# A macaron block with routed experts: a first stage of four tiles from one quarter of the tokens, and the front in another order

## The reference

```python
x = x + 0.5 * ffn(layernorm(x), ...)
x = x + attn(layernorm(x), ...)          # element [1] of it: a linear recurrence, 3 layers
x = x + 0.5 * ffn(layernorm(x), ...)

def ffn(x, Wr, br, ln_g, ln_b, W1, b1, W2, b2):        # E = 8 experts, D = 256, F = 1024
    router_probs = softmax(xt @ Wr + br)
    gates, idx = max(router_probs), argmax(router_probs)
    xn = layernorm(xt) * ln_g + ln_b
    h = relu(xn @ W1[idx] + b1[idx])
    return (h @ W2[idx] + b2[idx]) * gates
```

## Time and profile before

| what | value |
|---|---|
| median of 3 runs (lowest, highest) | 724.63 us (719.66, 725.75) |
| the profiled execution, its own time | 724.52 us |
| its span | 722.7 us |
| mean granted TensorE clock | 0.95 of full |
| PE busy, PEld busy | 665.7 us (92%), 582.8 us (81%) |
| DVE, ACT, POOL busy | 407.8, 269.7, 171.8 us |
| moved by DMA | 126.51 MB, 175 GB/s over the span |

### The profile page before, as it was taken

One profiled execution on the slowest core, in us unless ns is written; L12 is line 12 of the kernel. 1 busy time (PEld: TensorE's weight loads), 2 busy tenths in 40 slices (PEclk: granted clock), 3 DMA queues, 4 the chain that ended last, 5 costly groups with the idle time before them and its releaser, 6 DMA issues.

```text
span 722.7 us, 15480 instructions
## 1 busy us (share of the span) xinstructions
PE 665.7 (92%) x4414; PEld 582.8 (81%) x4414; DVE 407.8 (56%) x1415; ACT 269.7 (37%) x640; POOL 171.8 (24%) x177
## 2 busy tenths in 40 slices
PE   5748999799999999999998989999899989999993
PEld 4437899699997887888777867889699979999992
DVE  7356684233355667687787667787567623333331
ACT  3214222223234568453662546644343213222220
POOL 4452334111111111123412240123212511111111
PEclk8557999999999999999999999999999999999997
DMA  8897573765464552434515437333464465453540
GB/s 285 252 377 270 175 236 132 255 223 210 159 207 153 186 189 97 150 133 152 193 54 194 147 115 264 124 105 111 148 236 143 143 225 182 165 166 133 158 140 14
DMA packets 59919, 126.51 MB, mean 175 GB/s; under 512 B 8105, under 2 KB 36660, under 8 KB 59700
## 3 DMA queue, kind: packets, MB, share of 16 engines
q1 hardware_dynamic: 53204, 108.50, 44.6%
q0 software_dynamic: 6624, 16.92, 6.5%
HBM read 106.36 MB, written 20.35 MB: 175 GB/s over the span
## 4 chain that ended last, share of the span: by engine, by line
PE 63%; DVE 10%; issue 8%; SPq 5%; DVEq 4%; DMA 4%; POOL 2%; another core or an unknown queue 1%; ACT 1%; POOLq 0%; ACTq 0%
PE bank L1629 28%; PE bank L1643 26%; PE bank L1616 2%; SPq L403 2%; DMA pay<-routed_rows 2%; POOL routed_rows L609 2%; SPq L440 1%; PE bank L1533 1%; DVEq L391 1%; DMA routed_rows<-rows,dest 1%; DVE rec L1023 1%; PE bank L1566 1%; PE bank L1471 1%; DVE act_t L1113 1%
## 5 line engine op out<-in xcount | busy, mean ns | idle before, releaser
L1629 PE MATMUL bank<-mn_t,w 128*128 128x128 f32 x2368 | 286.4, 278 | 0.2
L1643 PE MATMUL bank<-w,act_t 128*128 x1184 | 280.5, 388 | 4.4 <-issue 2.2
L1629 PEld LDWEIGHTS bank<-mn_t,w 128*128 128x128 f32 x2368 | 276.4, 194 | 8.6 <-issue 7.2
L1643 PEld LDWEIGHTS bank<-w,act_t 128*128 128x128 f32 x1184 | 222.5, 194 | 42.9 <-issue 15.1
L1355 ACT ACTIVATE mn_t<-bank,vec 128x128 f32<-128x128 f32 x152 | 61.1, 452 | 239.7 <-PE bank L1616 226.7
L1113 DVE TENSOR_SCALAR act_t<-bank,vec 128x128 f32<-128x128 f32 x296 | 83.3, 344 | 108.7 <-PE bank L1629 94.1
L1365 ACT ACTIVATE act_t<-bank,vec 128x128 f32<-128x128 f32 x296 | 84.5, 367 | 79.2 <-PE bank L1629 77.9
L1122 DVE TENSOR_TENSOR y_b<-bank,b_all 128x256 f32<-128x256 f32 x74 | 31.4, 424 | 102.5 <-PE bank L1643 90.7
L618 POOL DMA_INDIRECT x_middle<-res,pay x37 | 38.0, 1027 | 213.6 <-DVE res L1128 188.4
L618 POOL DMA_INDIRECT out_x<-res,pay x37 | 37.0, 999 | 208.0 <-DVE res L1128 169.4
L609 POOL DMA_INDIRECT routed_rows<-rows,dest x64 | 63.6, 994 | 61.5 <-PE bank L1629 24.9
(11 more groups left out here) (200 smaller groups left out, 452.3 us busy)
## 6 DMA issues: line engine op xcount, KB each, us to landing
w<-in_L_ffn_W SPq DMA_DIRECT2D x82, 1024.0 KB
pay<-routed_rows SPq DMA_DIRECT2D x78, 130.0 KB, 2.1
rows<-in_L_attn_h SPq DMA_DIRECT2D x8, 512.0 KB, 7.3
rows<-x_middle SPq DMA_DIRECT2D x8, 512.0 KB, 4.6
routed_rows<-fill SPq DMA_DIRECT2D x2, 1040.0 KB
routed_rows<-rows,dest POOLq DMA_INDIRECT x64
b_all<-in_L_ffn_b SPq DMA_DIRECT2D x1, 1024.0 KB, 6.9
x_middle<-res,pay POOLq DMA_INDIRECT x37, 2.9
```

The lines of the kernel that those rows point to most:

```text
L1629: last = t.matmul(b_hid[half][:, c % 4 * P:(c % 4 + 1) * P], w1[i % W1S][:, k * F + c * P:k * F + (c + 1) * P], mn_t[p][i % 2][:, k * P:(k ...
L1643: last = t.matmul(b_out[i % 2], act_t[i % 2][:, c * P:(c + 1) * P], w2[:, ds(eb * (WE // FC) + c * D, D)], start=c == 0, stop=c == FC - 1)
```

## The change

FFN 0 gets three stages: 4 slots from chunk 0 alone, 5 from chunks 0 and 1, the rest from all. The first may also take partly filled tiles. Only the scatters of chunk 0 stand ahead of slot 0; those of chunk 1 and its table come between slots, as does the whole router of chunk 2 (transposes, logits, moments), which stood in the front. SP loads x of chunks 2 and 3 after everything that slots 0 to 2 need. The order of the loads changes: four second weights stand among the parameters, the filling of the regions of FFN 0 (`empty_rows(0)`) comes in the front instead of in slot 3, and slot 0's rows wait for it. `y_b` gets a second buffer, and PE's second product waits for its predecessor's bank to be read (`m_yk`) instead of for the result. All place lists are written anew. The highest possible number of slots of FFN 0 goes from 39 to 41.

```diff
-    FULL = -(-(TH - PART) // P)
-    EARLY = ((FULL,), (4, 9, 8))
-    UPTO = ((1, NC - 1), tuple(range(NC)))
+    EARLY = ((4, 5), (4, 9, 8))
+    UPTO = ((0, 1, NC - 1), tuple(range(NC)))
+    ANY = [(0, 0)] + [(1, s) for s in range(len(EARLY[1]))]
...
-R1_TRANSPOSE = [0, 48]
-R1_LOGITS = 192
+R1_TRANSPOSE = [[None, None], [None, None], [0, 48], [193, 288]]
+R1_LOGITS = [None, None, 192, 336]
-R_TURN_LOGITS = [[None, None, None, 216], [5952, 7368, 9696, 11256]]
+R_TURN_LOGITS = [[None, None, 264, 360], [6024, 8520, 10176, 11832]]
-R_SCATTER = [[[None, None, None, None], [None, None, None, None], [72, 120, 168, 216], [264, 312, 360, 408]],
-    [[1560, 1608, 1656, 1704], [2040, 2088, 2136, 2160], ...
+R_SCATTER = [[[None, None, None, None], [24, 25, 72, 74], [192, 193, 194, 312], [313, 360, 361, 408]],
+    [[1608, 1656, 1704, 1752], [2232, 2280, 2304, 2305], ...
...
 # SyncE, the front
             load_x(0, 1)
             sp.dma_start(rb_all[:, :], ...)
-            load_x(0, 2)
-            for e in range(E // 2):
+            load_parameters()                # second weights 0 to 3 after each 6 of its 24 loads
+            sp.wait_ge(s_c1, 3)
+            empty_rows(0)
+            for e in range(N_PAR // 6, E - 2):
                 second_weights(e)
-            load_parameters()
-            for e in range(E // 2, E):
-                second_weights(e)
-            load_x(0, 3)
             sp.wait_ge(s_tab, 1)
             slot_weights(0, 0)
-            for i in range(RING - 1):
+            for i in range(EARLY[0][0]):
                 next_rows(0, i)
+            for e in range(E - 2, E):
+                second_weights(e)
             slot_weights(0, 1)
             sp.dma_start(b2_all[:, :], ...)
             slot_weights(0, 2)
+            load_x(0, 2)
+            load_x(0, 3)
...
 # TensorE, second_product
-                        pe.wait_ge(m_r[p], i)
+                        pe.wait_ge(m_yk[p], i)
 # TensorE, the front
-            pe.wait_ge(s_c2, 1)
+            pe.wait_ge(s_c1, 1)
+            in_motion(7)
             for part in range(2):
                 transposes(R1, 0, part)
...
-            transposes(R1, 2, 0)
             ranks(0, 1)
-            transposes(R1, 2, 1)
             counts(0, 1)
-            logits(R1, 2)
-            parameters()
-            turn_logits(0, 2)
```

More of the change, by code:

```diff
@@ L33 @@
[L33 to L44, removed]
@@ L344, in macaron_block @@
         m_r = sems("result_ready", FFNS)
+        m_yk = [sem(f"product_read{p}") for p in range(FFNS)]
         m_s = [sems(f"result_stored{m}_", RING) for m in range(FFNS)]
@@ L568, in _ @@
             g.memset(ident[:, :], 0.0)
+            pool.drain()
+            g.affine_select(out=ident[:, :], in_=ident[:, :], compare_op=ALU.not_equal, fill=1.0, base=0,
+                            pattern=[[-1, P]], channel_multiplier=1).then_inc(s_c1, 1)
             g.memset(tri_f[:, :], 1.0)
             g.memset(ones_f[:, :], 1.0)
+            g.memset(pick[:, :], 0.0)
             g.iota(iota_i[:, 0:ENTRIES], [[1, ENTRIES]], base=0, channel_multiplier=0)
@@ L681, in _ @@
             powers(R1, 1)
-            for c in range(HC):
-                if c:
-                    pool.wait_ge(s_kept[R1], HC)
-                for part in range(NJ // 2):
-                    route(0, c, part)
+            for part in range(NJ // 2):
+                route(0, 0, part)
             first_pass()
@@ L839, in tables @@
                 classes = upto + 1 - c0
-                kinds = classes + (1 if f and not last else 0)
+                kinds = classes + int((f, s) in ANY)
                 m = kinds * E
@@ L864, in tables @@
                                                op0=ALU.add, op1=ALU.subtract)
-                    if f and not last:
+                    if (f, s) in ANY:
                         v.tensor_tensor(seg_x[:, E:2 * E], cnt_c[:, upto, :], done[:, :], ALU.subtract)
@@ L1213, in _ @@
             keep_counts(0, 0)
+            tables(0, 0, 0)
+            centre_down()
+            for part in range(1, 5):
+                tables(0, 0, part)
             choose(0, 1)
             place(0, 1)
-            centre_down()
             keep_counts(0, 1)
-            for part in range(5):
-                tables(0, 0, part)
             tables(0, 0, 5)
-            for b in range(NB):
-                moments(R1, 2, b)
             norm(0, 0)
@@ L1418, in _ @@
             keep_logits(R1, 0)
-            keep(R1, 1, 0)
+            for part in range(2):
+                keep(R1, 1, part)
             exponentials(0, 0)
-            keep(R1, 1, 1)
             keep_logits(R1, 1)
-            keep(R1, 2, 0)
+            parameters()
             exponentials(0, 1)
-            keep(R1, 2, 1)
-            keep_logits(R1, 2)
-            parameters()
             act.wait_ge(s_tab, 1)
```

145 lines of the change are left out of this document (81 added, 64 removed).

## The result

The changed kernel takes 741.86 us (median of 4 runs, 739.90 to 742.94), the kernel before 722.14 us in the same comparison. The ratio is 1.025 with a 95% interval of 1.021 to 1.029. The forecast was 731, its range 719 to 738: the sign was right, but 6.9 us were forecast and 19.7 came.

What follows compares the result with a forecast made beforehand. A 58 us front limited by transfers, then 665 us bound by PE's list. Terms -2.0 + 1.8 + 4.1 + 3.9 - 1.85 + 1.5 - 0.9 + 0.3 = +6.9 on 724.5 gave 731.4, said as 731; range 719 to 738.

Steps and rivals of the forecast that it cites:

- front, gate at x of chunk 2: Front: slot 0's rows come earlier, but PE waits for x of chunk 2 until 57.5 instead of 59.54: -2.0 us.
- low clock and moved router, up to slot 3: PE's early slots: low clock after the wait, +1.8, and chunk 2's router moved into PE's full list, +4.1.
- new start at slot 4: Added stage start at slot 4 of FFN 0 costs what slot 21 of FFN 1 showed: +3.9 us.
- slot 9: Stage start at slot 9 of FFN 0: last scatter a slot earlier, cost 3.9 instead of 5.75: -1.85 us.
- later lists, slot 4 of FFN 1: Slot 4 of FFN 1: new numbers put six scatters behind slot 3's first half: +1.5 us (0 to +3).
- skipped slots: Between the FFNs: two more possible slots, skipped, with their conditions: +0.3 us (0 to 1).
- read bank: PE's second product waits for the read bank instead of the result; half of 1.8 us of waits goes: -0.9.
- The first rival: The front's gain arrives, slot 0 starts 15 us earlier, PE not held by x of chunk 2: 716 us; chance 0.16.
- the second (725): Rival: new lists give back the moved work's cost by removing some 6 us of PE stalls: 725 us; chance 0.15.
- DVE's part: Chunk 2's router on DVE (moments, stage 1 tables) has room in slots 0 to 3: 0 us (up to +2).
- The low clock after the stand: PE after waiting for x of chunk 2: 7.5 us at low clock instead of 3.7, half lost: +1.8 (0 to +2.5).
- The third rival: Stage starts come late because chunk 1's scatters land after slot 3 begins: 737 us; chance 0.19.

Runs made afterwards that it cites:

- 15: Kernel before, with the changed kernel's later place lists and the recurrence's x loads of chunks 1 and 2 in slots 25 and 33: ratio 1.008.
- 18: Kernel before with 41 possible slots in FFN 0 instead of 39 (37 used), later places moved by two slots: ratio 1.0057.
- 4: Changed kernel, with PE's second product waiting again for the whole result of the slot before, not for the bank to be read: ratio 1.024.
- 10: Kernel before with only the two buffers of `y_b` and the read-bank wait added: ratio 0.998 (0.996 to 1.001).
- experiment 1: Changed kernel with x of chunk 2 issued early, behind second weights 4 and 5, instead of last but one: 736.5 us, ratio 1.017.
- Experiment 8: Changed kernel with the second half of chunk 3's moments on DVE in slot 1 of FFN 0 instead of slot 3: 738.4 us, ratio 1.020.
- experiment 11: Kernel before with only second weights 0 to 3 put among the parameter loads instead of ahead of them: 720.2 us, ratio 0.996.

## Why the prediction had the sign and not the size

| step | forecast | measured | by |
|---|---|---|---|
| front, gate at x of chunk 2 | -2.0 | -0.15 | 59.39 for 59.54 |
| low clock and moved router, up to slot 3 | +5.9 | +3.5 | first product of slot 3 |
| new start at slot 4 | +3.9 | +6.5 | first products |
| DVE behind in slots 5 and 6 | 0 | +1.9 | first products |
| slot 9 | -1.85 | -3.35 | first products |
| sum to slot 9 | +6.0 | +8.4 | ledger |
| later lists, slot 4 of FFN 1 | +1.5 | +6.9 | 15, ledger (runs: +5.6) |
| skipped slots | +0.3 | +3.9 | 18, slot 9 to 72 (runs: +4.1) |
| read bank | -0.9 | not told from 0 | 4, 10 |

The rows down to slot 9 come from the starts of first products. Slots 3, 5, 7, 8 and 9 were at 83.45, 98.08, 113.21, 120.24 and 137.05; they are at 86.81, 107.91, 124.96, 131.99 and 145.44. So they are 3.4, 9.8, 11.75, 11.75 and 8.4 us later: 3.4 - (-0.15) = 3.5, then 6.5 for the start, 1.9 between slots 5 and 7, where PE waits up to 1.73 us at a time for `y_b` of a DVE that is behind, and -3.35 at slot 9. Later lists and skipped slots make 10.8, where the ledger has 8.8 behind slot 9. A part is shared, since at the turn the moved pieces fill some of PE's empty time (3.23 for 4.25); the rest is within the ledger's noise.

**Right.** The gate, its place and length (12 us said, 13.08 seen); the four pieces of the moved router, which stand in slots 0 and 1 of PE's list (their price was not isolated: with the low clock 3.5 us up to slot 3, where 5.9 was said); that slot 9 gains; that the new start has a second product at the low clock. The first rival (716) is refuted, since the gain of 13 us did not arrive, and in experiment 1, where x of chunk 2 comes with the rest, PE waits for chunk 3 instead; the second (725) too, since the new lists cost instead of giving back.

**Wrong in size.** Two terms. The new start. I took 3.9 from slot 21 of FFN 1, where DVE is on time. Here the second half of chunk 3's moments stood on DVE ahead of it (from 93.56 to 95.7, with the slot's result at 96.84); I had put DVE's part at 0 (up to 2). Experiment 8 took that away, the idle time fell to 1.57 and the start to 3.9. Slot 9 gained 3.35 and not 1.85, since the clock stayed up at its start. The low clock after the stand (+1.8) cost about 0.7: the granted clock was 0.50 and 0.85 in the windows 62 to 64 and 64 to 66, for 0.70 and 1.00 before, and at 64.56 the transposes run at the full clock (1.05 us for 8), as before at 63.97. The front's term used 0.36 MB per us and a lull of 1.8 us. The lull was gone (369 GB/s from 55 to 57.5), but the mean rate was 341 GB/s, and so the wait ended 1.9 us later than said, within its bounds. Up to slot 3 the forecast's +3.9 and the measured +3.35 agree by luck: the gate gave back 1.85 less than said, and low clock and router cost 2.4 less. The rows of slot 0, said for 40.5 (55.2 - 15 is 40.2), came at 41.74.

**Wrong in kind.** Two steps failed, and they make most of the miss. The one at *slot 4 of FFN 1* named the scatters (+1.5, 0 to 3). The runs show instead that the later lists as a whole, with their loads, cost the kernel before 5.6 to 6.9 us, with PE's wait for a scan of the recurrence (2.5 to 4.5 us in the changed kernel and its variants) as the largest single one. The code shows that they belong to a weaker bound on tokens, by which x of chunks 1 and 2 is loaded two slots later; that the bound forces lists of this price was not shown. I had the line `FULL = -(-(TH - PART) // P)` in the diff, and followed what replaced it into the number of used slots but not into `WITH`. The other, *skipped slots* (+0.3, at most 1), named the right mechanism at a tenth of its price (+4.1 by the runs, 2.7 to 5.4): I counted conditions and looked for no row, while the turn of the FFNs in the trace of before (two skipped slots, 1.54 us idle and 5.37 for a first product that takes 3.7) would have bounded it. The third rival came nearest in time (737) with the wrong mechanism: at slot 4 DVE was late, and not the scatters of chunk 1.

What stays open: why DVE's wait called "remote" (2.73 us at 438.24) is long in some kernels and absent in others, and how much of the scan's wait is its doing. That lists for the later loads could be found that cost less is possible; only these and the old ones were run. Removing lists, two slots and the moved router brings the changed kernel to 1.0035; with the lists tried here the added stage thus gains nothing over the kernel before, and is 5 to 6 us behind experiment 11, which takes only the order of the loads.

## What to carry to other kernels

When a diff changes how much a stage is sure to process, follow that number into everything that is derived from it: here it moved loads by two slots, and the lists with them, and added two possible slots; together they cost about as much as all the edits at the front. A possible slot that is never used is not free when the engine that bounds the kernel has to walk over it. And an earlier start is worth only as much as the next transfer in the queue: here only large loads put between the small ones gained anything (0.4%).

## What the runs showed of the hardware

- 24 small parameter loads in a row held the transfers at 150 GB/s; with a 1 MB load after each six the same stretch moved 334 GB/s (changed kernel) and 364 (experiment 11).
- After the same idle time the clock may stay or fall. Idle 1.57 and 0.46 us at slot 4 in experiment 8, and 1.58 and 0.50 at slot 9 after, left 16 matmuls at 3.72 us; at slot 21 of FFN 1 before, after 1.56 and 0.47, they took 5.29. No run here tells why.

```profile
588.17 0.41 PE L1616 MATMUL bank<-ident,mn 128*128 128x128 f32 x2 [1.56 <-issue]
```

- The order of the fronts' loads was the same in all runs of one kernel, yet slot 0 of the kernel with 41 possible slots came 2.2 us earlier than that of the kernel before. Behind slot 9 the same code differed by up to 4.4 us between traces. Gains under 3 us are told by the medians of many runs, not by one trace.
